# Block 0 attention: three of four probability tiles turned by VectorE and DMA, normalised after the product of values

## The reference

```python
def _attn(q, k, v):
    ...
    scores = jnp.einsum('bhnd,bhmd->bhnm', q, k) * HD ** (-0.5)
    p = jax.nn.softmax(scores, axis=-1)
    o = jnp.einsum('bhnm,bhmd->bhnd', p, v)
...
h = _ln(x, ln1_w, ln1_b) * (1 + sc1[:, None, :]) + sh1[:, None, :]
qkv = h @ Wqkv + bqkv
q, k, v = jnp.split(qkv, 3, axis=-1)
x = x + _attn(q, k, v) @ Wos + bos
h = _ln(x, ln2_w, ln2_b) * (1 + sc2[:, None, :]) + sh2[:, None, :]
x = x + _attn(h @ Wq + bq, context @ Wk + bk, context @ Wv + bv) @ Woc + boc
```

## Time and profile before

| | before |
|---|---|
| median of 3 runs | 4015.68 us (4014.68 to 4016.24) |
| profiled run | 4010.95 us |
| its span | 4009.1 us |
| PE busy | 3839.5 us, 96% |
| DVE busy | 3157.0 us, 79% |
| ACT busy | 2468.4 us, 62% |
| POOL busy | 2862.1 us, 71% |
| HBM traffic | 101 GB/s over the span |

### The profile page before, as it was taken

How to read it: one execution, slowest core, us unless ns; L and a number is a source line. 1 busy time by engine, 2 the same in 40 slices (tenths; PEclk the granted TensorE clock), 3 DMA queues, 4 the chain that set the end, 5 groups by cost and what they waited for, 6 DMA issues and landing times.

```text
span 4009.1 us, 92934 instructions
## 1 busy us (share of the span) xinstructions
PE 3839.5 (96%) x32822; PEld 3295.7 (82%) x32822; DVE 3157.0 (79%) x6610; ACT 2468.4 (62%) x10244; POOL 2862.1 (71%) x2674
## 2 busy tenths in 40 slices
PE   7999999999989999999999999899999999999999
PEld 6777777777779997888888888788888888878998
DVE  7888889899985557888888888799998999975443
ACT  6999998898883334555555555455555555554333
POOL 5777877777767777666666666577777777766776
PEclk9999999999999999999999999999999999999999
DMA  2011111111111123777767677777777777772110
GB/s 81 28 33 33 33 46 41 41 49 49 54 40 54 43 64 102 219 210 219 216 212 223 208 222 225 215 213 235 223 231 222 226 231 225 231 227 85 52 43 32
DMA packets 415216, 544.98 MB, mean 136 GB/s; under 512 B 58524, under 2 KB 311968, under 8 KB 414752
## 3 DMA queue, kind: packets, MB, share of 16 engines
q1 hardware_dynamic: 267228, 404.74, 30.7%
q10 hardware_dynamic: 147524, 134.30, 12.9%
HBM read 220.11 MB, written 184.55 MB: 101 GB/s over the span
## 4 chain that ended last, share of the span: by engine, by line
PE 69%; DVE 12%; ACT 8%; DMA 4%; issue 3%; POOL 3%; ACTq 1%; SPq 0%; DVEq 0%
PE BANKS L621 17%; PE BANKS L622 15%; PE BANKS L623 15%; PE BANKS L780 6%; PE BANKS L768 5%; ACT PR L926 5%; PE BANKS L701 3%; PE BANKS L816 3%; DMA PB<-p_scratch 2%; DMA p_scratch<-TR 2%; PE BANKS L838 2%; DVE WL L1118 1%; DVE PT L1073 1%; POOL PR L1265 1%; DVE SN L1146 1%
## 5 line engine op out<-in xcount | busy, mean ns | idle before, releaser
L1265 POOL TENSOR_TENSOR PR<-PR,RL 128x512 f32<-128x512 f32 x1024 | 1064.1, 1042 | 602.9 <-DVE RL L1078 602.5
L942 ACT ACTIVATE PR<-BANKS,NM 128x128 f32<-128x128 f32 x2048 | 719.3, 378 | 334.5 <-DVE NM L1132 333.9
L926 ACT ACTIVATE PR<-BANKS,NM 128x128 f32<-128x128 f32 x2048 | 728.7, 414 | 12.7 <-DVE NM L1065 10.5
L621 PE MATMUL BANKS<-HH,WH 128*128 128x512 f32 x1632 | 681.4, 418 | 9.1 <-issue 7.4
L622 PE MATMUL BANKS<-HL,WH 128*128 128x512 f32 x1632 | 643.4, 394 | 0.0
L623 PE MATMUL BANKS<-HH,WL 128*128 128x512 f32 x1632 | 642.5, 394 | 0.0
L926 ACT ACTIVATION_READ_ACCUMULATOR PR<-BANKS,NM 128x1 f32 x2048 | 521.3, 255 | 0.0
L933 ACT ACTIVATE OH<-BANKS 128x512 fp32r<-128x512 f32 x256 | 153.1, 598 | 499.6 <-PE BANKS L768 257.8
L1132 DVE TENSOR_REDUCE NM<-BANKS 128x8 f32<-128x1024 f32 x256 | 310.4, 1213 | 190.4 <-PE BANKS L780 190.3
L942 ACT ACTIVATION_READ_ACCUMULATOR PR<-BANKS,NM 128x1 f32 x2048 | 445.5, 218 | 0.0
L621 PE MATMUL BANKS<-WH,OH 128*128 128x256 f32 x1280 | 375.6, 293 | 25.0 <-DVE OL L1150 20.8
(11 more groups left out here) (134 smaller groups left out, 10692.2 us busy)
## 6 DMA issues: line engine op xcount, KB each, us to landing
SW<-SN SPq DMA_DIRECT2D x1024, 128.0 KB, 2.9
p_scratch<-TR SPq DMA_DIRECT2D x256, 512.0 KB, 4.7
PB<-p_scratch ACTq DMA_DIRECT2D x1024, 128.0 KB, 3.8
x_scratch<-X SPq DMA_DIRECT2D x80, 512.0 KB, 3.2
X<-x_scratch SPq DMA_DIRECT2D x80, 512.0 KB, 4.3
CX<-in_ctx SPq DMA_DIRECT2D x32, 384.0 KB, 4.4
X<-in_x SPq DMA_DIRECT2D x16, 512.0 KB, 4.0
out<-X SPq DMA_DIRECT2D x16, 512.0 KB, 2.9
```

What stands on the lines that cost most here:

```text
L621: e.matmul(o, lh, rh, start=first and i == 0, stop=False)
L926: made = e.activation(pr[:, r], bank[:, r], ACT.Exp, bias=nm[:, h:h + 1], accum_out=RL[npr(t)[0]][:, h:h + 1])
L942: made = e.activation(pr[:, r], bank[:, r], ACT.Exp, bias=nm[:, h:h + 1], accum_out=RL[npr(t)[0]][:, h:h + 1])
L1265: e.tensor_tensor(p3, p3, RL[npr(t)[0]][:, :].unsqueeze(2).broadcast_to([128, 4, 128]), ALU.mult).then_inc(s_nrm, 1)
```

## The change

In passes 0 and 1:

- Tiles 0 to 2 of a batch (TURNED = 3) are no longer turned by TensorE. VectorE turns their 32x32 blocks into TR0 (stage "blocks0"), SP's queue writes the 768 KB to a scratch ("put0") and reads them back with four DMAs into PB0 ("get0"). Tile 3 is turned by TensorE and copied by ScalarE as before.
- No tile is normalised. The 16 sums of a batch stay in RL0; VectorE takes their reciprocals in one instruction and turns them in 32x32 blocks ("recip0"); SP's queue writes them to a scratch ("put_r") and reads them back spread over the 16 partitions of each head ("get_r", two DMAs with a repeated source). VectorE multiplies the product of values by them ("quot0"), to OF in SBUF. OH is written by ScalarE from OF, and OL by GpSimd instead of VectorE.
- Scale and shift of the tokens move from ScalarE to VectorE (stage "hf"), and HH from VectorE to GpSimd.
- The product of values and what follows it are three to four ticks later, the loads of X up to six ticks later, norms and q three ticks later, and pass 2 starts three ticks later. There is one more V buffer. Several waits guard buffers that now share memory between block 0 and block 1.

```diff
-NP0, NPT0 = 5, 6
+NP0, NPT0, NTR0, NPB0, NSC0, NV0 = 5, 2, 2, 2, 4, 4
+TURNED = 3
 NP1, NTR, NSW, NPT1, NSC = 4, 3, 3, 3, 4
...
-    T0[_p + 1] = END[_p] + {1: 0, 2: 2, 4: 0}.get(_p, 0)
+    T0[_p + 1] = END[_p] + {1: 3, 2: 2, 4: 0}.get(_p, 0)
 FIRST, LAST = T0[0] - 45, END[5] + 20
...
-            at["load_x", tg - {"a": 40, "b": 21, "f": 14}[kind]].append((p, g))
-            norm = tg - {"a": 26, "b": 12, "f": 8}[kind]
+            at["load_x", tg - ({"a": 40, "b": 21, "f": 14}[kind] if NG * p + g < NX or p > 1 else 34)].append((p, g))
+            norm = tg - {"a": 23 if (p, g) > (0, 1) else 26, "b": 12, "f": 8}[kind]
             turn = norm + {"a": 2, "b": 1, "f": 2}[kind]
             if (p, g) == (0, 1):
...
+                    tq += 2 * ((p, g) == (0, 1)) + 3 * ((p, g) > (0, 1))
...
-                for stage, tick in (("v", tb - 3), ("v_out", tb - 2), ("pv0", tb + 8), ("high0", tb + 9), ("low0", tb + 9),
-                                    ("out0", tb + 10), ("res0", tb + 11)):
+                for stage, tick in (("v", tb - 3), ("v_out", tb - 2), ("put0", tb + 4), ("get0", tb + 6), ("recip0", tb + 4), ("put_r", tb + 5), ("get_r", tb + 8),
+                                    ("pv0", tb + 11), ("quot0", tb + 12),
+                                    ("high0", tb + 13), ("low0", tb + 13), ("out0", tb + 14), ("res0", tb + 15)):
                     at[stage, tick].append(Batch(p, g, b))
                 for u in range(4):
                     t = Tile(n, p, ATT[p], g, b, u)
...
-                    for stage, lag in (("exp0", 0), ("normal", 1), ("p_turn", 3), ("p_copy", 4)):
+                    for stage, lag in (("exp0", 0),) + ((("blocks0", 1),) if u < TURNED else (("p_turn", 2), ("p_copy", 3))):
...
-                tp.add(("pv", x), FOUR, s_ol, 4 * xq(x.p, x.g) + x.b + 1)
+                tp.add(("pv", x), FOUR, s_of, 4 * xq(x.p, x.g) + x.b + 1)
...
+                for x in at["put0", tick]:
+                    vi = 4 * xq(x.p, x.g) + x.b
+                    q.wait_ge(s_tr0, TURNED * (vi + 1))
+                    q.wait_ge(s_pv0, vi - NSC0 + 1)
+                    e.dma_start(PSC0[vi % NSC0], TR0[vi % NTR0][:, :]).then_inc(s_put0[vi % NTR0], 16)
+                for x in at["get0", tick]:
+                    vi = 4 * xq(x.p, x.g) + x.b
+                    q.wait_ge(s_mods, 5)
+                    q.wait_ge(s_put0[vi % NTR0], 16 * (vi // NTR0 + 1))
+                    q.wait_ge(s_pv0, vi - NPB0 + 1)
+                    turned = PSC0[vi % NSC0].rearrange("(i c) (j k) -> j c i k", i=4, j=4)
+                    for j in range(4):
+                        e.dma_start(PB0[vi % NPB0][32 * j:32 * j + 32, :, :], turned[j]).then_inc(s_get0[vi % NPB0], 16)
+                for x in at["put_r", tick]:
+                    vi = 4 * xq(x.p, x.g) + x.b
+                    q.wait_ge(s_rt0, vi + 1)
+                    q.wait_ge(s_of, vi - NSC0 + 1)
+                    e.dma_start(RSC[vi % NSC0].rearrange("h (i c) -> i h c", i=4), RT0[vi % 2][:, :]).then_inc(s_put_r[vi % 2], 16)
+                for x in at["get_r", tick]:
+                    vi = 4 * xq(x.p, x.g) + x.b
+                    q.wait_ge(s_put_r[vi % 2], 16 * (vi // 2 + 1))
+                    q.wait_ge(s_of, vi - 1)
+                    for c in range(2):
+                        e.dma_start(RB[vi % 2][:, c, :], RSC[vi % NSC0, 8 * c:8 * c + 8].unsqueeze(1).broadcast_to([8, 16, T])).then_inc(s_get_r[vi % 2], 16)
...
-                    q.wait_ge(s_pt_d, 3 * vi + 3)
+                    q.wait_ge(s_get0[vi % NPB0], 64 * (vi // NPB0 + 1))
...
-                                made = e.matmul(bank[32 * r:32 * r + 32, 128 * c:128 * c + 128], V[vi % 3][:, 32 * h:32 * h + 32],
-                                                PT[(4 * vi + r) % NPT0][:, 128 * k:128 * k + 128], start=e_ == 0, stop=e_ == 1)
+                                o, v = bank[32 * r:32 * r + 32, 128 * c:128 * c + 128], V[vi % NV0][:, 32 * h:32 * h + 32]
+                                if r < TURNED:
+                                    k = 32 * (4 * r + k)
+                                    made = e.matmul(o.rearrange("p (i q) -> p i q", i=4), v, PB0[vi % NPB0][:, :, k:k + 32], start=e_ == 0, stop=e_ == 1)
+                                else:
+                                    made = e.matmul(o, v, PT[vi % NPT0][:, 128 * k:128 * k + 128], start=e_ == 0, stop=e_ == 1)
                     made.then_inc(s_pv0, 1)
...
                 for t in at["p_turn", tick]:
                     bank = PS[tp.bank(("p", t.n))]
-                    q.wait_ge(s_nrm, t.n + 1)
+                    q.wait_ge(s_exp, t.n + 1)
                     q.wait_ge(*tp.free(("p", t.n)))
...
-                    q.wait_ge(s_pv0, vi + 1)
+                    q.wait_ge(s_of, vi + 1)
                     q.wait_ge(s_mods, 5)
                     q.wait_ge(s_y, vi - 2)
-                    e.activation(OH[vi % 3][:, :, :], PS[tp.bank(("pv", x))][:, 0:256].rearrange("p (c t) -> p c t", c=2), ACT.Copy).then_inc(s_oh, 1)
+                    e.activation(OH[vi % 3][:, :, :], OF[vi % 3][:, :, :], ACT.Copy).then_inc(s_oh, 1)

...
                 for t in at["exp0", tick]:
                     q.wait_ge(s_nm0, t.n // 2 + 1)
-                    q.wait_ge(s_t, t.n - NP0 + 1)
-                    q.wait_ge(s_nrm, t.n - NP0 + 1)
+                    if t.n >= NP0:
+                        q.wait_ge(*consumed(t.n - NP0))
+                    q.wait_ge(s_vzero, NV0 + 3)
+                    q.wait_ge(s_rt0, t.n // 4 - 2)
                     bank, pr, nm = PS[t.u], PR[npr(t)[0]], NM0[t.n // 2 % 3][:, 4 * (t.n % 2):4 * (t.n % 2) + 4]
                     for h in range(4):
                         r = slice(128 * h, 128 * h + 128)
-                        made = e.activation(pr[:, r], bank[:, r], ACT.Exp, bias=nm[:, h:h + 1], accum_out=RL[npr(t)[0]][:, h:h + 1])
+                        made = e.activation(pr[:, r], bank[:, r], ACT.Exp, bias=nm[:, h:h + 1], accum_out=RL0[t.n // 4 % 3][:, 8 * (h // 2) + 2 * t.u + h % 2:8 * (h // 2) + 2 * t.u + h % 2 + 1])
                     made.then_inc(s_exp, 1)
...
                 for x in at["hf", tick]:
+                    if x.p < 2:
+                        continue
                     u, _ = h_of(x.p, x.g)
...
-                for t in at["p_copy", tick]:
-                    if t.u != 3:
-                        q.wait_ge(s_t, t.n + 1)
-                        q.wait_ge(s_mod, 3)
-                        q.wait_ge(s_pv0, npt(t)[1] // 4 + 1)
-                        e.tensor_copy(PT[npt(t)[0]][:, :], PS[tp.bank(("p", t.n))][:, :]).then_inc(s_pt_d, 1)
+                for t in at["blocks0", tick]:
+                    vi = t.n // 4
+                    q.wait_ge(s_exp, t.n + 1)
+                    if vi:
+                        q.wait_ge(s_mods, 5)
+                    q.wait_ge(s_put0[vi % NTR0], 16 * (vi // NTR0))
+                    e.transpose(TR0[vi % NTR0][:, :].rearrange("p (j k c) -> p j k c", j=4, c=32)[:, :, 4 * t.u:4 * t.u + 4, :],
+                                PR[npr(t)[0]][:, :].rearrange("p (h j c) -> p j h c", h=4, j=4)).then_inc(s_tr0, 1)
+
+                for x in at["quot0", tick]:
+                    vi = 4 * xq(x.p, x.g) + x.b
+                    bank = PS[tp.bank(("pv", x))]
+                    q.wait_ge(s_pv0, vi + 1)
+                    q.wait_ge(s_get_r[vi % 2], 32 * (vi // 2 + 1))
+                    q.wait_ge(s_ol, vi - 2)
+                    e.tensor_tensor(OF[vi % 3][:, :, :], bank[:, 0:256].rearrange("p (c t) -> p c t", c=2), RB[vi % 2][:, :, :], ALU.mult).then_inc(s_of, 1)
+
+                for x in at["recip0", tick]:
+                    vi = 4 * xq(x.p, x.g) + x.b
+                    q.wait_ge(s_exp, 4 * vi + 4)
+                    e.reciprocal(RL0[vi % 3][:, 0:16], RL0[vi % 3][:, 0:16]).then_inc(s_rl0, 1)
+                    q.wait_ge(s_rl0, vi + 1)
+                    q.wait_ge(s_put_r[vi % 2], 16 * (vi // 2))
+                    e.transpose(RT0[vi % 2][:, :], RL0[vi % 3][:, :]).then_inc(s_rt0, 1)

...
-                for x in at["low0", tick]:
-                    vi = 4 * xq(x.p, x.g) + x.b
-                    q.wait_ge(s_oh, vi + 1)
-                    e.tensor_tensor(OL[vi % 3][:, :, :], PS[tp.bank(("pv", x))][:, 0:256].rearrange("p (c t) -> p c t", c=2), OH[vi % 3][:, :, :].bitcast(F),
-                                    ALU.subtract).then_inc(s_ol, 1)

...
+                for x in at["hf", tick]:
+                    if x.p > 1:
+                        continue
+                    u, _ = h_of(x.p, x.g)
+                    bank = PS[tp.bank(("turn", x))]
+                    q.wait_ge(s_mods, x.p + 1)
+                    q.wait_ge(s_turn, hparts["turn", x] + 1)
+                    q.wait_ge(s_hl, 2 * u + x.c - 3)
+                    for b in range(2 * x.i, 2 * x.i + 2):
+                        r, bb = slice(128 * b, 128 * b + 128), G * x.g + b
```

(21 more changed lines are left out.)

63 lines of the change are left out of this document (42 added, 21 removed).

## The result

The changed kernel takes 4039.19 us (median of four runs, 4037.71 to 4041.42) against 4015.18 us of the kernel before: ratio 1.0061, 95% interval 1.0044 to 1.0079. It is 0.6% slower where 1.7% faster was forecast. The profiled run has a span of 4037.4 us.

A forecast was written before the change was run, and what follows sets the result against it. No engine alone bounded block 0's attention; engines 85 to 93% full were coupled. Pass 0 gains 51 us, pass 1 24, tail costs 4: net -71, 3940, or 3945 against the median; 3905 to 3985 at 0.57, range 3895 to 4060.

The forecast's parts named there:

- What bounds the kernel: Block 0's attention: no engine alone at the limit; exponentials, reciprocals, products, turns and copies wait along engines 85 to 93% full.
- the part on TensorE: Block 0: 12 of 16 turns per batch go, 8.16 us becomes about 7.1; nothing charged for the clock.
- The pace that follows: Block 0 with VectorE fullest at 95.5%: 7.76 us per batch, taken as 7.9, in pass 0; 8.72 in pass 1.
- rival (a): Engines stay coupled as tightly, VectorE at 92.8%: 7.99 and 8.98 us per batch, 3968 us; chance 0.57 shared with forecast.
- VectorE: Block 0, per batch: terms sum to +0.06 (to +0.22) us; 7.35 becomes 7.41 in pass 0, 8.27 becomes 8.33 in pass 1.
- ScalarE and GpSimd: Block 0, per batch: ScalarE from 8.07 and 8.13 us to 7.4; GpSimd from 6.9 to 4.0.
- SyncE and DMA: SP's queue in block 0: put0 lands in 5.5 us, loop 7.6 us per batch, hardly below VectorE's 7.76 in pass 0.
- (b): SP's put and get loop sets block 0's pace: about 3990 us (mild, 0.10) or 4110 at long landings (0.11).
- (c): A few DMA engines fill up with block 0's tile and reciprocal transfers, middle 9.3 us per batch: 4071 us; chance 0.08.
- Moved steps and seams: Later X load may lose up to 1 us per group, inside the range; q projection still precedes its scores; prologue 0.
- The tail: Block 0's end: FFN starts three ticks later, put and get precede the last product; +4 us (0 to 10).
- Rival (d): Block 0's maxima wait as before, pace stays 8.7 and 9.1 us: 4015 to 4022; chance 0.07 shared with (b) near even.

The follow-up runs named there:

- hf_act: The changed kernel with scale and shift of the tokens back on ScalarE, HH staying on GpSimd: 4033.03 us, ratio 1.0060 to the kernel before.
- fill12: The changed kernel with tile 3 turned four times over, 12 redundant TensorE turns more per batch of block 0: 3992.93 us, ratio 0.9964.
- fill_b3: The changed kernel with 12 redundant turns only for the last batch of each group: 4032.43 us, ratio 1.0046.
- place_nor: `place` with the reciprocals left out, so block 0 is not normalised: 3984.38 us, ratio 0.9932.
- place_late: `place` with quot0 moved behind the low parts of q and k in VectorE's order: 4017.98 us, ratio 1.0015.
- place: The changed kernel with redundant turns of tile 3 only at TensorE's long waits, placed separately for each pass: 3995.93 us, ratio 0.9959.
- late: The changed kernel with only quot0 moved behind the low parts of q and k in VectorE's order: 4116.55 us, ratio 1.0264.

## Why the prediction was wrong, step by step

*What bounds the kernel*: read rightly. The failing step that turned the sign is in the part on TensorE: "at 7.1 of some 8 us it still works without long pauses, so I charge nothing for the clock". The load was right (257.70 us for 34.5 batches is 7.5 with slowed products in it, and `hf_act`, at a clock of 0.99, has 245.08 us, 7.1), the conclusion was not. A busy share says nothing of how the rest is spread: TensorE's slack came largely in waits of 1.2 to 2.1 us ahead of the score products, where before the longest such wait was 0.4 us in the stretch of pass 0 and 0.6 in that of pass 1. I had written a granted clock below 1.00 in block 0 as something that would prove me wrong, and gave it no rival and no price. It costs some 44 us, from 1157.3 to 1113.4 with `fill12`.

*The pace that follows.* With the clock held, pass 0 runs at 8.37 to 8.48 us, forecast 7.90, and pass 1 at 8.86 to 8.93, forecast 8.72. This is the second failing step, 30 to 37 us in pass 0 and 9 to 13 in pass 1. It is the larger one in size: the profiled `fill12` has a span 15.0 us below that of the kernel before (3994.1 against 4009.1), where 71 were forecast, so even without the clock 56 us of the forecast gain were not there. The start was also misread a little: 9.09 us per batch for pass 1 came from a count in one stretch, the 56 batches have 8.99, which takes 6 us off the 24 that the sum gave to pass 1. In pass 1 the share taken, 95.5%, is what came (285.48 of 300, 95.2%); in pass 0 VectorE reaches 90.4% in `fill12` and 91.2% in `fill_b3`. There rival (a), engines coupled as tightly as before, was nearer, and even its 92.8% and 7.99 us were too good. What makes up this coupling was tried with `place_nor` and `place_late` and not settled.

*VectorE.* The terms were small in size and partly wrong. From the changed kernel, first the groups of 750 to 1050, then the timeline:

```profile
L1132 DVE STREAM_TRANSPOSE TR<-PR 128x512 f32<-128x512 f32 x95 | 64.9, 696 | 0.2
L1264 DVE TENSOR_SCALAR HF<-BANKS,MODS,MODB 128x128 f32<-128x128 f32 x64 | 22.6, 395 | 0.0
...
L1141 DVE TENSOR_TENSOR OF<-BANKS,RB 128x256 f32<-128x256 f32 x32 | 13.5, 422 | 24.2 <-PE BANKS L798 24.2
```

```profile
833.09 0.69 DVE L1264 TENSOR_SCALAR HF<-BANKS,MODS,MODB 128x128 f32<-128x128 f32 x2
833.70 0.70 DVE L1132 STREAM_TRANSPOSE TR<-PR 128x512 f32<-128x512 f32 x1
...
838.34 0.24 DVE L1146 RECIPROCAL RL<-RL 128x16 f32<-128x16 f32 x1
838.62 0.21 DVE L1149 STREAM_TRANSPOSE RT<-RL 128x32 f32<-128x32 f32 x1
838.76 1.18 DVE L1123 TENSOR_REDUCE NM<-BANKS 128x8 f32<-128x1024 f32 x1
```

Scale and shift take 0.395 us each, 0.31 start to start, where L1097's 0.19 was taken and 0.27 was the upper bound: 0.62 per batch instead of 0.38. The nearest row by size was not the nearest by kind: this one reads two columns of scalars (that they are the reason is not shown). The reciprocal pair takes 0.42, forecast 0.30. The stream transpose is right (0.696 against 0.680), quot0 is 0.03 longer. Together VectorE has 7.64 us per batch in pass 0 and 8.45 in pass 1, forecast 7.41 and 8.33.

*ScalarE and GpSimd.* 259.14 us are 7.5 per batch, forecast 7.4; GpSimd 3.8, forecast 4.0 (its copy of 128x512 takes 0.61, not 1.0).

*SyncE and DMA*: right. put0 lands in 5.4 us in the median (3.5 to 8.3), forecast 5.5, a get issues in 0.432 us and lands in 4.0. In pass 0 SP waits 59.1 us for put0's landing and still 22.9 for VectorE's turns, so its loop is not full. Tile PB over both passes, what TensorE's and VectorE's idle time ahead of its users ended with, and then the same for RB:

```profile
  issue: 31.5, 102
  DMA PB<-p_scratch: 3.5, 4
...
  PE BANKS L798: 94.5, 62
  DMA RB<-r_scratch: 1.0, 1
```

In these 1140 us the engines waited 3.5 us for tiles and 1.0 us for reciprocals. Rivals (b) and (c) did not happen. The rule of the Trainium skill on outermost dimensions below 16 ("DMA: Bandwidth & Descriptors", Rules for kernel authors) could not be seen in the time: the DMA share is 0.81, and taking these transfers away gave 11 us with the clock held, VectorE's pair included.

*Moved steps and seams.* The later X load costs nothing that shows. The tail was forecast at +4 and is +0.5 (+2.1 in `fill12`, +3.5 in `place`). The start was forecast at 0 and is +4.2.

*Rival (d)* gave nearly the number of pass 0 (8.7, measured 8.62), but for another reason: the waits for turns were gone from VectorE, and a new loss of nearly the same size had come. That these two nearly cancel is chance.

## What to carry to other kernels

Before taking work off TensorE, ask how its waits will lie, not how full it stays: find where it will now wait longest and what it does right behind that wait, and price that stretch at the lower clock (here 0.42 us for a product instead of 0.23). When a change that lightens an engine brings nothing, look at the granted clock in stretches of 2 us, and give TensorE redundant work ahead of its longest waits as a test; if that is faster and the granted clock rises with it, the clock was the loss. Take a pace over whole groups: a count in a stretch of 300 us hid that pass 0 was faster and pass 1 slower than it seemed. In a chain this tightly coupled an edit that delays TensorE can cost a multiple of itself, as `late` and `place_late` show.
